# Attention on one Trainium2 core: k, q, the row maxima and the mask turned by transposing DMA transfers instead of TensorE

## The reference

```python
q = _layernorm(x)                 # 16 x 256 x 256, 16 heads of 16
k = v = ctx_1024                  # 16 x 256 x 256
scores = einsum('bqhd,bkhd->bhqk', q, k)
scores = where(mask == 0, -1e20, scores)
attn = softmax(scores / 256 ** 0.5)
x = x + einsum('bhqk,bkhd->bqhd', attn, v).reshape(b, l, e) @ W_out.T + b_out
```

## Time and profile before

| | |
|---|---|
| median of 3 runs | 1388.85 us |
| the profiled execution's own time | 1396.29 us |
| its span, first to last instruction | 1394.4 us |
| busy in the span: TensorE, VectorE, ScalarE, GpSimd | 89%, 63%, 46%, 41% |
| attention, first to last scores on TensorE | 20.1 to 370.6 us |
| DMA share of the whole span, hardware queue q1 | 39.8% |

### The profile page before, as it was taken

One profiled execution on the slowest core, in us unless ns is written; L12 is line 12 of the kernel. 1 busy time (PEld: TensorE's weight loads), 2 busy tenths in 40 slices (PEclk: granted clock), 3 DMA queues, 4 the chain that ended last, 5 costly groups with the idle time before them and its releaser, 6 DMA issues. The chain is left out here.

```text
span 1394.4 us, 29774 instructions
## 1 busy us (share of the span) xinstructions
PE 1237.5 (89%) x10841; PEld 934.3 (67%) x10852; DVE 882.6 (63%) x2642; ACT 641.1 (46%) x1097; POOL 574.5 (41%) x604
## 2 busy tenths in 40 slices
PE   3799999999847798997579999966999999999996
PEld 1355555554422466886468988855989999989995
DVE  5888888887779672225465576533666566665663
ACT  2588787877454571224126532312333333333331
POOL 5656765676252005996100004561333333333333
PEclk9999999999959999999888999987999999999999
DMA  6212222213141004650339105226888887888782
GB/s 224 54 64 82 92 92 78 92 53 127 40 131 53 0 1 129 203 180 31 121 97 239 39 5 190 99 90 205 250 258 249 255 253 239 258 251 253 245 244 67
DMA packets 104193, 196.40 MB, mean 141 GB/s; under 512 B 15632, under 2 KB 86928, under 8 KB 91552
## 3 DMA queue, kind: packets, MB, share of 16 engines
q1 hardware_dynamic: 89792, 178.21, 39.8%
q0 software_dynamic: 14304, 16.93, 5.7%
HBM read 144.70 MB, written 52.23 MB: 141 GB/s over the span
## 5 line engine op out<-in xcount | busy, mean ns | idle before, releaser
L2016 PE MATMUL banks<-moe_w,moe_hT 128*128 128x256 f16 x2640 | 296.9, 273 | 0.0
L2016 PEld LDWEIGHTS banks<-moe_w,moe_hT 128*128 128x128 f16 x2640 | 258.3, 98 | 30.0
L1927 ACT ACTIVATE moe_hf<-banks,moe_b 128x256 f32<-128x256 f32 x440 | 184.5, 471 | 170.8 <-PE banks L2003 170.8
L1871 POOL DMA_INDIRECT out_x<-moe_y,slot_owner x78 | 121.6, 1559 | 285.9 <-DVE moe_y L2249 256.5
L747 DVE CUSTOM_DVE_ANT_0 masked<-banks,mask_bias 128x256 f32<-128x256 f32 x512 | 193.2, 420 | 37.4 <-PE banks L518 37.3
L2003 PE MATMUL banks<-moe_rT,moe_w 128*128 128x256 f16 x1872 | 212.7, 274 | 0.0
L2003 PEld LDWEIGHTS banks<-moe_rT,moe_w 128*128 128x128 f16 x1872 | 184.3, 98 | 21.8
L2136 DVE TENSOR_TENSOR moe_hT<-moe_hf,moe_hT 128x512 f16<-128x512 f32 x220 | 154.1, 700 | 7.6
L409 ACT ACTIVATE probsT<-banks 128x1024 f32<-128x1024 f32 x128 | 131.1, 1025 | 47.1 <-PE banks L549 45.1
L1857 POOL DMA_INDIRECT slots_x<-moe_xn,pos x64 | 64.1, 1002 | 158.9 <-DVE pos L2200 123.4
L1911 ACT ACTIVATE moe_rT<-banks 128x512 f16<-128x512 f32 x39 | 23.3, 597 | 213.3 <-PE banks L1988 213.3
(11 more groups left out here) (322 smaller groups left out, 1967.2 us busy)
## 6 DMA issues: line engine op xcount, KB each, us to landing
moe_w<-moe_halves SPq DMA_DIRECT2D x80, 1024.0 KB, 5.0
moe_halves<-half_parts SPq DMA_DIRECT2D x18, 1024.0 KB, 8.5
slots_x<-empty_row SPq DMA_DIRECT2D x1, 10140.0 KB, 51.4
moe_rows<-slots_x SPq DMA_DIRECT2D x39, 260.0 KB, 5.9
half_rows<-in_L_ffn_Wfc SPq DMA_DIRECT2D x8, 1024.0 KB, 6.4
half_rows<-in_L_ffn_Wproj SPq DMA_DIRECT2D x8, 1024.0 KB, 6.6
moe_b<-in_L_ffn_bproj SPq DMA_DIRECT2D x39, 128.0 KB, 5.4
ctx_rows<-in_ctx SPq DMA_DIRECT2D x16, 256.0 KB, 2.8
```

The costliest lines, as they stand in the source:

```text
L1871: pool.indirect_dma_start(out=out_rows, out_offset=bass.IndirectOffsetOnAxis(ap=owner[:, s, t:t + 1], axis=0), in_=y[s % 2][:, t, :], in_o ...
L1927: ins = act.activation(hf[p][:, j, :], src, ACT.Gelu_apprx_tanh, bias=b1[buffer][:, j:j + 1], scale=1.0 / WSCALE)
L2016: ins = pe.matmul(OUT[p][:, t * D:(t + 1) * D], hT[p][:, x, j, t * P:(t + 1) * P], w2[buffer][:, w, j, :], start=(j == 0 and (w, x) == PAR ...
```

## The change

SP turns the operands with `dma_start_transpose`, from SBUF to SBUF, and copies the swapped mask halves with plain DMA. All 60 TensorE transposes of k, q, maxima and mask go, with the copies on ScalarE and VectorE, and `ident16`. TensorE has at most one operation beside scores and mask in a slot (two in slot 5): `project` is cut in two, one half in the next step, and `out_turn` and `project` write `psum_m`. SP's list is written out by step. `set_live`, `set_mask`, `normalise`, `add`, `split_max` and `see_mask` get new slots on VectorE, behind both `take_max` of a slot; GpSimd does `values` ahead of `split_q`. In step 13 SP's list has the weights of the MLP, 2180 KB, which it issued after the last step before.

```diff
+            def turn_k(b):
+                sp.wait_ge(s_k, 3 * b + 3)
+                if b >= 1:
+                    sp.wait_ge(s_kT, 32 * b)
+                if b >= 3:
+                    sp.wait_ge(s_ST, HP * (b - 2))
+                for t in range(NQ):
+                    sp.dma_start_transpose(kT[b % 3][:, :, t * P:(t + 1) * P],
+                                           k_split[b % 2][:, t, :, :, :].rearrange("p h a e -> p (h a e)")).then_inc(s_kT, 16)
+            def turn_q(b):
+                sp.wait_ge(s_q, 3 * b + 3)
...
+            def turn_max(b, half):
+                sp.wait_ge(s_mp, 2 * (2 * b + half + 1))
...
+                for t in range(NQ):
+                    sp.dma_start_transpose(qmT[b % 2][:, pairs, t * P:(t + 1) * P],
+                                           q_split[b % 2][:, t, half * HP:(half + 1) * HP, :, :].rearrange("p h a e -> p (h a e)")).then_inc(s_qm[half], 16)
+            def turn_mask(b):
+                sp.wait_ge(s_mb, b + 1)
...
+                for t in range(NQ):
+                    sp.dma_start_transpose(mask_biasT[b % 2][:, 0, :, t * P:(t + 1) * P], mask_bias[b % 2][:, t, :]).then_inc(s_mT, 16)
+            def swap_mask(b):
+                sp.wait_ge(s_mT, 32 * (b + 1))
+                for half in range(2):
...
+                    sp.dma_start(mask_biasT[b % 2][here, 1, :, :], mask_biasT[b % 2][there, 0, :, :]).then_inc(s_swap, 16)
...
+            for n in range(2):
+                load_half(sp, d, w, n)
+            for B in PHASES:
+                if real(B):
+                    turn_max(B, 1)
+                if real(B + 1):
+                    turn_mask(B + 1)
+                if real(B + 2):
+                    turn_k(B + 2)
+                    turn_q(B + 2)
+                if real(B + 1):
+                    swap_mask(B + 1)
+                if 2 <= B + 3 < NB:
+                    load_ctx(B + 3)
+                if 2 <= B + 4 < NB:
+                    load_mask(B + 4)
+                if B % 2 and 2 <= (B + 3) // 2 < CUT_BESIDE_ATTENTION:
+                    store_half(sp, w, halves_dram, (B - 1) // 2)
+                    load_half(sp, d, w, (B + 3) // 2)
+                if B == NB - 3:
...
+                if real(B + 1):
+                    turn_max(B + 1, 0)
 def split_k(b):
-                    pool.wait_ge(s_fillT, 4 * (b - 2) + 2)
+                    pool.wait_ge(s_kT, 32 * (b - 1))
 def split_q(b):
-                    pool.wait_ge(s_rT, 2 * (b - 2) + 2)
+                    pool.wait_ge(s_qm[0], 32 * (b - 1))
+                    pool.wait_ge(s_qm[1], 32 * (b - 1))
 def scores(b, hp, j, t):
-                    pe.wait_ge(s_fillA, 3 * b + 3)
-                    pe.wait_ge(s_fillV, b + 1)
+                    pe.wait_ge(s_kT, 32 * (b + 1))
+                    pe.wait_ge(s_qT, 32 * (b + 1))
 def scoresT(b, hp, j, k):
-                    pe.wait_ge(s_r, 2 * b + hp // (HP // 2) + 1)
+                    pe.wait_ge(s_qm[hp // (HP // 2)], 32 * (b + 1))
 def scoresT_mask(b, hp):
-                    pe.wait_ge(s_m, b + 1)
+                    pe.wait_ge(s_swap, 32 * (b + 1))
 def out_back(b, t):
+                if t == 0 and b >= 1:
+                    pe.wait_ge(s_xadd, b)
+                if t == 1:
+                    pe.wait_ge(s_on, NQ * b + 1)
             for B in PHASES:
                 for hp in range(HP):
                     both_scores(B, hp, 0)
...
                     both_scores(B, hp, 1)
                     if real(B):
                         scoresT_mask(B, hp)
+                    if hp == 0 and real(B - 2):
+                        project(B - 2, 1)
                     if hp == 1 and real(B - 1):
+                        weigh(B - 1, 3)
+                    if hp == 2 and real(B - 1):
                         out_back(B - 1, 0)
+                    if hp == 3 and real(B):
+                        weigh(B, 0)
+                    if hp == 4 and real(B - 1):
+                        out_back(B - 1, 1)
+                    if hp == 5 and real(B):
+                        weigh(B, 1)
+                    if hp == 5 and real(B - 1):
+                        out_turn(B - 1)
+                    if hp == 6 and real(B - 1):
+                        project(B - 1, 0)
+                    if hp == 7 and real(B):
+                        weigh(B, 2)
```

On VectorE, behind `take_max(B + 1, hp, 0)` and `take_max(B + 1, hp, 1)` of a slot:

```diff
+                    if hp == 0 and real(B + 2):
                         set_live(B + 2)
+                    if hp == 1 and real(B - 2):
+                        add(B - 2)
+                    if hp == 2 and real(B - 1):
+                        normalise(B - 1, 0)
+                    if hp == 3 and real(B + 2):
+                        set_mask(B + 2)
+                    if hp == 4 and real(B - 1):
+                        normalise(B - 1, 1)
+                    if hp == 5 and real(B + 1):
                         split_max(B + 1, 0)
+                    if hp == 6 and real(B + 3):
                         see_mask(B + 3)
+                        see_rows_live(B + 3)
+                    if hp == 7 and real(B + 1):
+                        split_max(B + 1, 1)
```

More of the change, by code:

```diff
@@ new lines, in turn_mask @@
+            def turn_mask(b):
+                sp.wait_ge(s_mb, b + 1)
+                if b >= 1:
+                    sp.wait_ge(s_swap, 32 * b)
+                if b >= 2:
+                    sp.wait_ge(s_ST, HP * (b - 1))
+                for t in range(NQ):
+                    sp.dma_start_transpose(mask_biasT[b % 2][:, 0, :, t * P:(t + 1) * P], mask_bias[b % 2][:, t, :]).then_inc(s_mT, 16)
+            def swap_mask(b):
+                sp.wait_ge(s_mT, 32 * (b + 1))
+                for half in range(2):
+                    here, there = slice(HALF_P * half, HALF_P * (half + 1)), slice(HALF_P * (1 - half), HALF_P * (2 - half))
+                    sp.dma_start(mask_biasT[b % 2][here, 1, :, :], mask_biasT[b % 2][there, 0, :, :]).then_inc(s_swap, 16)
@@ L295, in _ @@
             sp.dma_start(woT[:], d["wo0T"].rearrange("(k p) e -> p k e", p=P)).then_inc(s_x[2], 16)
[L297 to L311, removed]
+            w, mlp = g.cut, g.mlp
@@ L578, in out_turn, with project @@
                         at = (t * 2 + k) * P
-                        ins = pe.transpose(psum_o[:, at:at + P], o_rows[t][:, k * P:(k + 1) * P], ident[:])
+                        ins = pe.transpose(psum_m[:, at:at + P], o_rows[t][:, k * P:(k + 1) * P], ident[:])
                 ins.then_inc(s_oTp, 1)
-            def project(b):
-                pe.wait_ge(s_oT, b + 1)
-                if b == 0:
-                    pe.wait_ge(s_x[2], 80)
-                for t in range(NQ):
-                    for k in range(2):
-                        ins = pe.matmul(psum_o[:, t * D:(t + 1) * D], oT[:, t, k, :], woT[:, k, :], start=(k == 0), stop=(k == 1))
-                ins.then_inc(s_op, 1)
+            def project(b, t):
+                if t == 0:
+                    pe.wait_ge(s_oT, b + 1)
+                    if b == 0:
+                        pe.wait_ge(s_x[2], 80)
+                for k in range(2):
+                    ins = pe.matmul(psum_m[:, t * D:(t + 1) * D], oT[:, t, k, :], woT[:, k, :], start=(k == 0), stop=(k == 1))
+                if t == NQ - 1:
+                    ins.then_inc(s_op, 1)
             for B in PHASES:
@@ L776, in add @@
                 v.wait_ge(s_bias, b + 1)
-                v.tensor_tensor(X[:, T, :], X[:, T, :], psum_o.rearrange("p (t c) -> p t c", t=NQ), ALU.add).then_inc(s_xadd, 1)
+                v.tensor_tensor(X[:, T, :], X[:, T, :], psum_m.rearrange("p (t c) -> p t c", t=NQ), ALU.add).then_inc(s_xadd, 1)
             def see_weights():
@@ L818, in _ @@
                     if (B, hp) in AHEAD:
[L819 removed]
+                        v.wait_ge(s_xadd, NB - 3)
                         see_rows(v, g, X, *AHEAD[B, hp])
[L822 to L825 removed]
                     if B == -2 and hp == 5:
```

210 lines of the change are left out of this document (40 added, 170 removed).

## The result

The changed kernel takes **1426.63 us** (median of 4 runs, 1423.22 to 1432.46) against 1389.76 us of the kernel before beside it (4 runs, 1385.22 to 1394.77): ratio 1.027, 95% interval 1.022 to 1.032. It is slower. 1401 us were forecast, in a range of 1350 to 1500.

The account below looks back on a forecast made before the run. TensorE was taken to bound the attention steps at 20.27 us, VectorE 3.3 us behind. Terms -29.4 + 17.6 + 9.2 + 1 - 0.5 + 14 = +11.9 us on 1388.85 gave 1401 us, range 1350 to 1500.

Parts of the forecast that it names:

- The mechanism: Attention steps alternate at about 16.6 and 23 us; TensorE idles some 7 us before even steps until DMA fills `qmT`.
- step 13: The MLP's 2180 KB also go ahead of the maxima on SP, adding 6.3 us to 2.9: +9.2 us.
- TensorE at 15.6 us: TensorE's work in an attention step without the removed transposes: 20.27 - 4.66 = 15.6 us.
- VectorE at 16.3 us plus 0.3 of waiting: VectorE loses one 0.69 us copy and bounds even steps at 16.6 us, 3.67 less each, -29.4 us over eight.
- The packets at 24 ns: DMA transposes: 6656 packets of 256 bytes a step at 24 ns each, 10 us a step.
- Quick packets: Rival: transposes take 4.8 us a step, odd step 20.8 us, the clock holds; 1370 us, chance 0.16.
- dear ones: Rival: packets cost 49.5 ns and the DMA bounds the attention; +88 us, 1477 us, chance 0.16.
- The odd step at 23.2 us: Maxima queue behind two megabytes of weights on SP; odd steps grow 2.9 us, +17.6 us over steps 1 to 11.
- The even step at 18.6 us: Even step of 16.6 us bound by VectorE, plus 2.0 us for TensorE's lowered clock after each gap (+14 in all).
- The start: Batch 0's transposes wait behind two weight loads; first scores move from 20.1 to about 28 us, costing +1 us.
- SP as the bound: Rival: issuing a transpose takes SP 2.52 us, deciding from 1.4 us; steps of 27.5 us, 1497 us, chance 0.16.
- no block: Rival: maxima don't stand behind the weights, so every step takes 16.6 us; 1334 us, chance 0.12.

Follow-up runs that it names:

- the hybrid: Changed kernel with the maxima's transposes back on TensorE and two ScalarE copies a step; k, q and mask still turned by DMA: 1361.59 us, ratio 0.978.
- the spread run: Changed kernel with the weight store kept in odd steps and the load moved to even ones, each behind the second half of the maxima: 1392.09 us, ratio 1.000.
- sooner: The spread run with the maxima's first half sent directly behind q and written by VectorE in slot 4 instead of 5: 1377.73 us, ratio 0.991.

## Why the prediction was right, and where it was off

**The mechanism** was the forecast's. Steps of two lengths came, TensorE stood idle 6.6 to 11 us ahead of even steps and was released by a DMA into `qmT`, and the first matmuls behind the gaps took 0.39 us. Spreading the weights (-35 us) and taking the maxima out of the DMA (-65 us) show the cause by experiment.

**The sum** did less well than the mechanism. The forecast added 12 us and 37 came; direction and range held, and the range is 150 us wide. In the attention of the two profiled executions, each step read from its first transposed scores to those of the next:

| | forecast, us | measured, us |
|---|---|---|
| start | +1 | +4.9 |
| even steps 0 to 14, clock and last steps' -0.5 included | -15.9 | -5.1 |
| odd steps 1 to 11 | +17.6 | +34.8 |
| step 13 | +9.2 | +8.5 |
| from step 15 to the MLP's weights | 0 | -1.1 |
| sum | +11.9 | +42.0 |

**TensorE at 15.6 us** held: the hybrid's steps have (16.02 + 17.23) / 2 = 16.6 us with two of the removed groups, 1.1 us, back in them.

**VectorE at 16.3 us plus 0.3 of waiting** was mis-sized. The hybrid shows 17.44 us busy and a step of 17.9. The small operations, counted as unchanged, grew; the groups of VectorE between 60 and 380 us in the hybrid (count, busy, mean ns):

```profile
L695 DVE TENSOR_SCALAR mask_bias<-mask_all,row_live 128x256 bf16<-128x256 bf16 x28 | 14.6, 564 | 0.0
L715 DVE TENSOR_SCALAR q_split<-row_max 128x16 f16<-128x16 f32 x30 | 13.0, 432 | 0.5
L717 DVE SCALAR_TENSOR_TENSOR q_split<-row_max,q_split 128x16 f16<-128x16 f32 x30 | 12.2, 408 | 1.0
L688 DVE TENSOR_TENSOR live_shift<-nmr,row_live 128x2 f32<-128x2 f32 x13 | 9.6, 739 | 0.0
```

and the same groups in the kernel before:

```profile
L759 DVE SCALAR_TENSOR_TENSOR q_split<-row_max,q_split 128x16 f16<-128x16 f32 x30 | 7.9, 262 | 1.0
L731 DVE TENSOR_SCALAR mask_bias<-mask_all,row_live 128x256 bf16<-128x256 bf16 x26 | 6.2, 281 | 0.0
L757 DVE TENSOR_SCALAR q_split<-row_max 128x16 f16<-128x16 f32 x30 | 6.2, 206 | 0.5
L724 DVE TENSOR_TENSOR live_shift<-nmr,row_live 128x2 f32<-128x2 f32 x13 | 2.0, 154 | 0.0
```

Together they took 49.4 us against 22.3 in these 320 us; the conversion of the mask, 857 ns before and 421 in the hybrid, gave 5.6 us of it back. So the gain of an even step that VectorE bounds is 20.27 - 17.9 = 2.4 us, not 3.67.

**The packets at 24 ns** agree with the mean of all (24.7), but that mean has the longer packets of the loads in it. The turned ones took 20.7 ns when nothing else moved, 6656 x 20.7 / 16 = 8.6 us a step and not 10; of the quarter more for the turning little was there. That the 19.5 ns came so near is luck: 163 of the 284 packets of the earlier trace rows are under 512 bytes and 121 are of 512 or more, and 0.25 KB is only their mean. Quick packets (4.8 us a step) and dear ones (49.5 ns) are both ruled out.

**The odd step at 23.2 us** was 26.1 in the mean of the six (24.2 to 27.4). The one shown took 25.8, by its own stations: q parts ready at 7.8 us into the step (8.1 forecast), q issued at 9.0 (9.2), the second half of q landed some 4.7 after that, at 13.8 (12.3); context, mask, store and load at 24.7, by the load's issue at 14.7 and its landing 10.0 us later (20.8); the maxima 1.1 later (2.4 forecast). The failing term is the one for two megabytes: 6.6 us were taken from the earlier trace rows, where no turned packets moved beside them, and it was about 10, with the end of q, context and mask ahead. The sentence that "it is the queue they wait in" holds of the DMA engines and not of SP's queue.

**The even step at 18.6 us**, clock included, was 20.1 in the mean of the six from 2 to 12 (20.1, 19.8, 21.0, 21.3, 19.4 and 18.7). TensorE's work under the low clock was sized rightly (18.51 us busy, 15.6 + 2.9 = 18.5 forecast), and the 2.0 us that the clock was to cost a step lie within the 1.2 to 2.4 of the two steps that kept it. What the forecast lacked is the way of the maxima in a step without weights. It put their writing at about 12 us into a step; in the one that begins at 101.6 us VectorE ended it at 117.25, 15.7 us in, SP issued them at 117.74, and they landed at 121.7, when TensorE's wait of 1.00 us for them ended:

```profile
117.02 0.23 DVE L695 SCALAR_TENSOR_TENSOR q_split<-row_max,q_split 128x16 f16<-128x16 f32 x1
```

The step ended with that way, with TensorE's work done; why VectorE writes the maxima so late no run took apart.

**The start** was +4.9 instead of +1: the first scores came at 31.83 us, not at 28, and the first transpose, issued at 16.38 us behind the weight loads, took SP 8.15 us.

**SP as the bound** was priced at 2.52 us a transpose and decided from 1.4; it is 1.24 to 1.33 in the median, so it doesn't bound the steps by itself. Yet once the block is removed, *no block* (1334 us) doesn't follow: the spread run stands at 1392. Of the 58 us between, the larger VectorE accounts for 15 x 1.3 = 20; the way of the maxima from VectorE's slot 5 through SP and the transpose to the next step for 14 (`sooner`). Of the other 24 some 3 are the start (52.76 us to the first transposed scores in the spread run); for the rest no run decides. The queues, near full in the last runs, are a candidate, and the clock, at 0.92 in two steps of the spread run, another. The forecast costed the maxima as hidden by slots 5 to 7; their way takes 189.9 (written) to 195.0 us (landed) in the spread run, and TensorE needed them at 193.4.

## What to carry to other kernels

Work that is moved off a bounding engine is only free if its new way is short against the slack of the value that it carries: k, q and the mask have about a step of slack and gained by DMA, the maxima have some 3.5 us and lost. Beside a bulk transfer a small urgent one waits for it, whether it stands behind it in the queue or in another queue; put time or distance between them, or keep the urgent value on a compute engine. And when the bounding engine is relieved, read again the small operations of the next one: their durations are not constants.

## What the runs showed of the hardware

- A transposing DMA from SBUF to SBUF costs its issuer a median of 1.24 us at 64 KB (mask), 1.27 at 128 KB (half of the maxima) and 1.33 at 256 KB (k); a plain one 0.43 to 0.60 us. With the engines full the four transposes of the maxima held SP for 9 to 10 us, and one of k at the start for 8.15.
- It lands 2.4 us (64 KB) to 3.3 us (256 KB) after issue on quiet queues; half of the maxima 2.4 us where nothing stood before it, 10.9 us at most where the weights did. This is the view of SP's transposes into `qmT` in the changed kernel:

```profile
L308 SPq DMA_TRANSPOSE qmT<-q_split x48: 1190/1268/3424, 70.4 to 329.9; - x48
...
DMA to landing us min/median/max: 2.4/3.8/10.9
```

- Small operations of VectorE end together with an operation of GpSimd that runs beside them. Of the 30 operations `q_split<-row_max` of the hybrid (line 715) 16 took over 0.3 us, and each of the 16 ended within 0.12 us of one of GpSimd's; of the 30 in the kernel before none took over 0.3 us. In the timelines of the two engines (start, length) the first ends at 176.32 and 176.26 us, the second at 184.36 and 184.35:

```profile
175.56 0.76 DVE L715 TENSOR_SCALAR q_split<-row_max 128x16 f16<-128x16 f32 x1
...
183.24 1.12 DVE L688 TENSOR_TENSOR live_shift<-nmr,row_live 128x2 f32<-128x2 f32 x1
```

```profile
175.10 1.16 POOL L156 TENSOR_TENSOR half_parts<-half_rows,half_parts 128x512 f16<-128x512 f32 x1
...
183.19 1.16 POOL L156 TENSOR_TENSOR half_parts<-half_rows,half_parts 128x512 f16<-128x512 f32 x1
```

  The Trainium skill (SBUF — State Buffer, SBUF: two separate sides) says that the two engines share one pair of ports as an exclusive lock, so that for certain operations of VectorE the later one waits for the whole operation of the other. These rows agree; which slots of VectorE meet GpSimd's work changed with the slots' order, and no run here moved them apart to see the 1.3 us come back.
